# Value products of the first cross attention in three pieces per octet instead of four

## The reference

```
q = layernorm(x) @ wq + bq          # 16 x 64 x 128
k = ctx @ wk + bk ; v = ctx @ wv + bv   # 16 x 1601 x 128
att = softmax(q_h k_h^T / sqrt(8))  # per batch and head: 64 x 1601
x = x + concat_h(att v_h) @ wo + bo
```

## Time and profile before

| what | value |
|---|---|
| median of 3 runs | 1681.71 us (1681.11 to 1683.48) |
| the profiled execution's own time | 1684.89 us |
| its span in the profile | 1683.0 us |
| TensorE busy over the span | 1578.0 us (94%) |
| VectorE, ScalarE, GpSimd busy | 1261.1, 957.8, 699.3 us |
| steps of the first cross attention | about 39 to 521 us |

### The profile page before, as it was taken

How to read it: one execution, slowest core, us unless ns; L and a number is a source line. 1 busy time by engine, 2 the same in 40 slices (tenths; PEclk the granted TensorE clock), 3 DMA queues, 4 the chain that set the end, 5 groups by cost and what they waited for, 6 DMA issues and landing times. The chain is left out here.

```text
span 1683.0 us, 34753 instructions
## 1 busy us (share of the span) xinstructions
PE 1578.0 (94%) x13494; PEld 1406.1 (84%) x13494; DVE 1261.1 (75%) x2816; ACT 957.8 (57%) x1788; POOL 699.3 (42%) x962
## 2 busy tenths in 40 slices
PE   6999999999997899799999999999999999999864
PEld 4777777777776788689999999999999999999843
DVE  7677777777773788578788788777887877777587
ACT  3566666666663334366566566565666666656452
POOL 3132232222301354166646655474656564661110
PEclk9999999999998899999999999999999999999985
DMA  6543563644520012300000000010100010100000
GB/s 165 126 109 99 118 169 80 137 99 102 116 60 24 1 51 95 110 32 14 33 22 32 25 23 33 21 33 14 34 20 33 14 33 20 34 1 2 1 3 10
DMA packets 32547, 90.40 MB, mean 54 GB/s; under 512 B 8536, under 2 KB 17408, under 8 KB 32384
## 3 DMA queue, kind: packets, MB, share of 16 engines
q1 hardware_dynamic: 32384, 88.18, 19.8%
HBM read 39.90 MB, written 8.91 MB: 29 GB/s over the span
## 5 line engine op out<-in xcount | busy, mean ns | idle before, releaser
L385 DVE TENSOR_TENSOR c_p_lo<-c_turn_ps,c_p_hi 128x512 fp32r<-128x512 f32 x384 | 264.4, 689 | 143.1 <-ACT c_p_hi L336 136.2
L336 ACT ACTIVATE c_p_hi<-c_turn_ps 128x512 fp32r<-128x512 f32 x384 | 228.1, 594 | 242.0 <-PE c_turn_ps L248 241.0
L1055 DVE TENSOR_REDUCE a_chunk_max<-a_side_ps 128x1 f32<-128x512 f32 (+1 forms) x416 | 260.6, 665 | 89.8 <-PE a_side_ps L799 89.1
L354 ACT ACTIVATE c_prob<-c_score_ps,c_neg_max 128x836 f32<-128x836 f32 (+1 forms) x256 | 245.2, 958 | 29.8 <-DVE c_neg_max L423 26.7
L376 DVE TENSOR_REDUCE c_chunk_max<-c_score_ps 128x1 f32<-128x836 f32 (+2 forms) x384 | 256.9, 721 | 3.5 <-PE c_score_ps L278 3.5
L248 PE MATMUL c_turn_ps<-consts,c_prob 128*128 128x128 f32 (+1 forms) x1792 | 244.3, 274 | 6.7 <-DVE c_p_lo L385 6.4
L966 ACT ACTIVATE a_prob<-a_st_ps 128x1024 f32<-128x1024 f32 (+1 forms) x224 | 214.0, 958 | 59.4 <-PE a_st_ps L783 59.2
L248 PEld LDWEIGHTS c_turn_ps<-consts,c_prob 128*128 128x128 f32 (+1 forms) x1792 | 207.0, 140 | 25.1 <-DVE c_p_lo L385 12.7
L799 PE MATMUL a_side_ps<-a_stack,a_q_bd 96*128 96x512 f32 (+1 forms) x512 | 160.5, 390 | 12.0 <-DVE a_q_bd L1065 3.0
L783 PE MATMUL a_st_ps<-a_q_bd,a_stack 100*128 100x256 f32 (+1 forms) x832 | 151.7, 302 | 1.3 <-DVE a_q_bd L1065 1.2
L2529 POOL CAST c_rden_hi<-c_rden 128x4 fp32r<-128x4 f32 x32 | 6.0, 187 | 353.7 <-DVE c_rden L399 353.7
(11 more groups left out here) (391 smaller groups left out, 3783.1 us busy)
## 6 DMA issues: line engine op xcount, KB each, us to landing
a_stack<-a_k_hi SPq DMA_DIRECT2D x128, 200.1 KB, 4.1
a_stack<-a_k_lo SPq DMA_DIRECT2D x64, 200.1 KB, 4.2
a_ctx<-in_ctx_dram SPq DMA_DIRECT2D x16, 768.0 KB
ctx_rows<-in_ctx_dram SPq DMA_DIRECT2D x16, 768.0 KB
c_q_raw<-absorbed_queries SPq DMA_DIRECT2D x15, 512.0 KB, 3.3
absorbed_queries<-b_q_out SPq DMA_DIRECT2D x8, 512.0 KB, 3.1
absorbed_queries<-last_queries SPq DMA_DIRECT2D x8, 512.0 KB, 3.1
w<-in_L_ffn_w_dram SPq DMA_DIRECT2D x2, 512.0 KB
```

Source lines behind the costliest of these rows:

```text
L336: last = nc.scalar.activation(p_hi[u][:, 4 * c:4 * c + 4, P * j:P * j + P], turn_ps[c % 2][:].rearrange("p (t q) -> p t q", t=4), ACT.Copy)
L354: nc.scalar.activation(prob[s % 2][:, probs_of[c]], score_ps[:, cols], ACT.Exp, bias=neg_max[:, s % 2:s % 2 + 1], accum_out=sums[:, (s // ...
L385: last = nc.vector.tensor_tensor(p_lo[u][part], turn_ps[c % 2][:].rearrange("p (t q) -> p t q", t=4), p_hi[u][part].bitcast(F32), ALU.subt ...
L1055: nc.vector.reduce_max(out, rows, AX_X).then_inc(side_taken, 1)
```

## The change

The value products of steps 0, 1, 2 are issued together at step 3, those of 3, 4, 5 at step 6, and those of step 6 at step 0 of the next octet as before. A fourth buffer `prob` (1024 x 4 bytes a partition) is added, so an exponential waits for the value products 4 steps before. "den" moves from step 2 to step 3, behind the value products there.

```diff
@@ -461,6 +461,7 @@
 V_COLS = 17
+PROBS = 4
@@ -498,7 +499,7 @@ def small_product_at(n, s):
-    if s == 2 and n > 0:
+    if s == 3 and n > 0:
         return ("den", n - 1)
@@ -563,7 +564,7 @@
-        prob = [sb(f"prob{i}", [P, 2, BANK]) for i in range(3)]
+        prob = [sb(f"prob{i}", [P, 2, BANK]) for i in range(PROBS)]
@@ -830,7 +831,7 @@ def weigh_values(t):
-                                                prob[t % 3][0:rows, i, P * j:P * j + P], start=(2 * s + i == 0), stop=(2 * s + i == FULL))
+                                                prob[t % PROBS][0:rows, i, P * j:P * j + P], start=(2 * s + i == 0), stop=(2 * s + i == FULL))
@@ -942,9 +943,9 @@
                     if s == 0 and n:
                         weigh_values(n * STEPS - 1)
-                    elif s % 2 == 0 and s:
-                        weigh_values(n * STEPS + s - 2)
-                        weigh_values(n * STEPS + s - 1)
+                    elif s % 3 == 0 and s:
+                        for before in (3, 2, 1):
+                            weigh_values(n * STEPS + s - before)
@@ -956,13 +957,13 @@ def exponent(n, s):
-                if t >= 3:
-                    act.wait_ge(pv_done, t - 2)
+                if t >= PROBS:
+                    act.wait_ge(pv_done, t - PROBS + 1)
```

More of the change, by code:

```diff
@@ L958, in exponent @@
                 act.wait_ge(scored, t + 1)
-                if t >= 3:
-                    act.wait_ge(pv_done, t - 2)
+                if t >= PROBS:
+                    act.wait_ge(pv_done, t - PROBS + 1)
                 if len(step_tiles[s]) == 2:
-                    out, scores = prob[t % 3][:], st_ps[t % 2][:]
+                    out, scores = prob[t % PROBS][:], st_ps[t % 2][:]
                 else:
                     rows = step_tiles[s][0][0]
-                    out, scores = prob[t % 3][0:rows, 0, :], st_ps[t % 2][0:rows, 0, :]
+                    out, scores = prob[t % PROBS][0:rows, 0, :], st_ps[t % 2][0:rows, 0, :]
                 nc.scalar.activation(out, scores, ACT.Exp).then_inc(exp_done, 1)
```

## The result

The changed kernel takes 1718.93 us (median of 4 runs, 1717.21 to 1719.65) against 1682.6 us for the kernel before in the same comparison: a ratio of 1.0204, 95% interval 1.0184 to 1.0223. It is 36 us slower. I had forecast 23 us slower, and 1718.93 lies above my range, which ended at 1712.

What follows compares the result with a forecast made beforehand. TensorE's written order was taken to pace the stage, pieces covering VectorE's work on the side banks. Even octets +7.5, odd +18.6 less 1.0, octets 29 and 30 +0.8, octet 31 -0.3, DMA -2.2 gave +23.4: 1705.1 us, range 1691 to 1712.

Steps and rivals of the forecast that it cites:

- The clock falls: Rival: new idle stretches of 0.7 to 1.3 us bring TensorE from 2.4 to 1.2 GHz; 1752 us, chance 0.03.
- odd octet, no q0: Odd octets without job q0: late k1 1.04, longer step 6 piece 0.44, less 0.15 at the maxima; +1.33 us each.
- odd octet with q0: Octets 1, 3, 5, 7: job q0 in step 2 shields part of the wait, 0.25 us less than other odd octets.
- odd: k1 to shift: Odd octets, step 4: a chain not touching the piece keeps 3.11 us, so removing the piece is worth 0.
- even octet: Octets 0 to 28: step 2's lost piece becomes a wait ahead of shift, step 6's piece grows 0.44; +0.50 us each.
- waits ahead of unit 12, of shift (odd, even): TensorE loads idle 0.8 us at unit 12 of step 3, over 1 us at shift in odd octets, 0.6 in even.
- "issue" ahead of L832: Idle weight loads for "issue" ahead of value products fall to some 90 from 117 times.
- octets 29, 30, 31: Last octets: 29 and 30, without a k job, +0.4 us each by estimate; 31, without maxima, saves one edge, -0.3.
- waits for DMA: Three waits for stack DMAs, 2.2 us, shrink as octets lengthen; -2.2 us.
- sum without the clock: All octet terms and DMA waits together: +23.4 us, median 1705.1 us; chance 0.74 for its own range 1696 to 1711.
- The edges decide: Rival: VectorE's work is early enough, so one saved piece edge per octet gives 9.0 us, 1672.7; chance 0.08.
- Only the long chain costs: Rival: even octets break even, odd ones lose about half, +7 us, 1689; chance 0.11.

Runs made afterwards that it cites:

- run 12: The changed kernel with three prob buffers instead of four (PROBS = 3); ratio 1.0187 to the kernel before.
- run 1: The changed kernel with five spare 512-column products in the wait ahead of shift, step 4 of odd octets up to 27; 1708.84 us, ratio 1.0134.
- run 5: Kernel before with four prob buffers; even octets give the piece of step 6 to step 0 of the next octet; ratio 0.9999.
- run 9: Kernel before with den at step 3 up to octet 27 and step 6's piece moved to step 0 behind it for even octets 10 to 26; 1678.75 us, ratio 0.9944.
- run 7: Kernel before with only den moved to step 3 and a fourth prob buffer, four pieces kept; ratio 0.9975.
- run 8: Kernel before with only the fourth prob buffer added, schedule unchanged; ratio 1.0001.
- run 10: The changed kernel with shift moved from step 4 to step 6, behind the piece of three steps; ratio 1.0211.
- run 3: Three pieces and den at step 3 in even octets only, odd octets as in the kernel before; ratio 1.0021.

## Why the prediction was wrong

**The step that failed** is the rival "The clock falls" and what I set against it. I gave it 0.03 and left its cost out of the range. My argument was a row: in the last octet PE is busy for 5.24 of 6.00 us with the clock at 1.00. That is a mean over an octet, and a mean says nothing of how the idle time lies: octet 25 kept its clock at 13.67 of 15.84 us, less than that share, while octet 27, with the same instructions and waits, lost it. In the last octet PE's idle time comes in bits of under 0.4 us; in octet 27 of the changed kernel loads wait 0.95 us ahead of unit 12 and, a step later, 1.62 us ahead of shift. Its place was right (idle stretches of 0.7 to 1.3 us), its chance too low and its price too high: I took a tenth of the stage, 47 us of products, at the low clock and 47 us of cost; measured are eight stretches of some 3.5 us, 1.5 us each, 12 us in all. It was no rival to my forecast but an addition to it: had I added those 12 us, the sum would have been 1717.

**The rest, step by step, against the octets of clock 1.00.**

| step of the prediction | forecast | measured |
|---|---|---|
| odd octet, no q0 | +1.33 | +1.39 |
| odd octet with q0 | +1.08 | +1.11 |
| odd: k1 to shift | 3.11, unchanged | 3.10 |
| even octet | +0.50 | +0.32 |
| piece of three steps to the next product | 1.44 | 1.43 to 1.44 |
| octet pair | 32.0 | 31.85 (15.84 + 16.01) |
| waits ahead of unit 12, of shift (odd, even) | 0.8; over 1; 0.6 | 0.73; 1.22; 0.56 |
| "issue" ahead of L832 | some 90 times | 53 times, 17.2 us |
| octets 29, 30, 31 | +0.4, +0.4, -0.3 | +2.25 (+0.92 in run 12, at clock 1.00), -0.06, +0.29 |
| waits for DMA | -2.2 | 2.2 to 0.7, -1.5 |
| sum without the clock | +23.4, 1705.1 us | run 1: 1.0134, 1705.1 us |

That the last line agrees to a tenth is luck. Its interval is 1702.3 to 1708.0 us, it still holds a clock fall in octet 29, and errors cancel in my sum: the even octets are 0.18 us shorter than forecast, some 2.7 us in 15, while the DMA waits gave back less and octets 29 and 31 cost more. The mechanism of the waits stands on the octets, not on this figure.

- *Even octets*: v2 behind den takes 0.81 us to the scores (253.51 to 254.32), not 0.92 as behind unit 12, so the maxima and shift came 0.1 us earlier than I had them.
- *The count of "issue"* was wrong because I counted one piece less per octet. But where unit 12 has waited (463.33 above), the loads of the piece behind it show no idle entry at all.
- *Octet 31*: I gave it the edge it saves. It is paced by ScalarE's exponentials (TensorE idles 0.34 and 0.64 us for two of them), and the piece of three steps at step 3 comes later than one of two at step 2.
- *The edges decide* fell: the loads' idle time for "issue" did shrink by 20 us, but the waits for maxima ahead of shift alone grew by 31 us. *Only the long chain costs* had the right place (the odd octets) and half the size.
- *The two places from the Trainium skill.* The Trainium skill, TensorEngine Tiling (Array Packing), Key Properties, on the drain at a change of mode: runs 5 and 9 show what an edge is worth where nothing waits behind it: 0.35 us an octet pair in which one is saved (15.35 against 15.70 in run 5, 15.28 in run 9 against 15.64 in run 7), near the 0.38 expected of run 5 (0.28 for the edge, 0.1 for a wait). That some cost stands at the edge is thus borne out; whether it is the drain the rows can't tell. The Trainium skill, Perfetto Trace Analysis, Optimization Strategy, on repeating bubbles as a sign of too few buffers: the buffer in SBUF is worth nothing (run 8, 1.0001, and run 12), and in run 10 the wait moves to the next user of the side banks. Both fit a shortage of side banks in PSUM, but a third bank was not tried, so this is argued and not shown.

Not settled: why the clock falls in some odd octets and not in others with the same waits (5, 7, 9, 13, 15, 19, 27 in one execution, 3, 9, 15, 17, 21, 23, 27 in run 12's), and what decides that run 3's waits of 1.0 us leave it alone. In run 10, where the long wait ahead of shift is gone, it fell in octets 2, 10 and 31 only.

## What to carry to other kernels

Work that looks like overhead on the busiest engine may be the cover under which another engine's chain runs. Before merging pieces of it, follow what stands behind each piece to its last releaser: if it already waits with the piece in place, taking the piece away gains nothing there, and the work comes back whole where it is put. Merge only where the trace shows no such wait close behind, as in run 9. And if a change adds idle stretches of about a microsecond on TensorE, put a price on the clock beside the wait; it added half as much again here (12 us on some 23), and spare products in the gap took it away.

## What the runs showed of the hardware that was not expected

- TensorE's granted clock fell from 1.00 to 0.50 (1.2 instead of 2.4 GHz) in seven of the 14 odd octets up to 27, while octets with the same waits kept it; in octet 27 idle loads of 0.95 us (495.18) and 1.62 us (500.52) came ahead of a stretch from 502.4 to about 506 us. Each time 1.5 us were lost. With five spare products of 0.23 us in the second gap none of the 14 octets lost its clock (run 1).
- A value piece in four column groups costs 0.0275 us a record and 0.12 us at its end, taken from pieces of 8 records (0.34 us) and 32 (1.00 us) before; the piece of 48 after takes 1.43 to 1.44 us, by this line 1.44.
